# Layer 0 in one-pass products, experts batch by batch: a two-layer kernel with attention and experts

## The reference

```python
qkv = einsum('bsd,ed->bse', xn, w_qkv) + b_qkv      # 16 heads of 16
attn = softmax(q k^T / 4 + causal); s = (attn v) @ w_out.T + b_out
logits = xn @ router_w.T                            # 8 experts, best 2
w = softmax(top2(logits))
gate  = silu(einsum('nd,edf->enf', xn, w1))         # 256 -> 128
value = einsum('nd,edf->enf', xn, w2)
expert_out = einsum('enf,efd->end', gate * value, w3)
f = sum over the two chosen experts of w * expert_out
```

## Time and profile before

| | us |
|---|---|
| median of 3 runs | 1393.04 |
| lowest, highest | 1392.79, 1396.16 |
| the profiled execution, its own time | 1396.62 |
| its span in the profile | 1394.9 |
| mean granted TensorE clock | 0.979 |

### The profile page before, as it was taken

One profiled execution on the slowest core, in us unless ns is written; L12 is line 12 of the kernel. 1 busy time (PEld: TensorE's weight loads), 2 busy tenths in 40 slices (PEclk: granted clock), 3 DMA queues, 4 the chain that ended last, 5 costly groups with the idle time before them and its releaser, 6 DMA issues. The chain is left out here.

```text
span 1394.9 us, 33366 instructions
## 1 busy us (share of the span) xinstructions
PE 1317.5 (94%) x12564; PEld 1086.2 (78%) x12564; DVE 1119.6 (80%) x2294; ACT 946.3 (68%) x2605; POOL 847.0 (61%) x966
## 2 busy tenths in 40 slices
PE   6999999878999999999999999999999999999985
PEld 3554445667898989898888888889888888888884
DVE  4495646898989888979788988878888878887875
ACT  3105574467787878777877777868777777777664
POOL 8011124338866777576767677577776867676652
PEclk9998999989999999999999999999999999999997
DMA  9910001213111121121121111121112222113011
GB/s 323 167 32 2 5 1 46 77 42 99 39 28 43 35 87 42 28 80 36 39 74 40 41 31 41 43 69 53 27 47 62 62 62 54 55 51 88 17 54 38
DMA packets 61592, 78.84 MB, mean 57 GB/s; under 512 B 6232, under 2 KB 48856, under 8 KB 61432
## 3 DMA queue, kind: packets, MB, share of 16 engines
q1 hardware_dynamic: 56696, 62.41, 17.2%
q0 software_dynamic: 4736, 14.29, 3.7%
...
## 5 line engine op out<-in xcount | busy, mean ns | idle before, releaser
L2029 ACT ACTIVATE XY<-ps 128x512 f16<-128x512 f32 x384 | 219.3, 597 | 64.7 <-PE ps L1274 56.8
L1777 DVE TENSOR_TENSOR ZL<-ps,cst 128x256 f16<-128x256 f32 x384 | 152.3, 415 | 32.3 <-PE ps L1261 27.6
L1687 DVE SCALAR_TENSOR_TENSOR yv<-ps,cw,yv 128x511 f32<-128x511 f32 (+2 forms) x192 | 143.3, 746 | 14.9 <-ACT yv L1966 10.0
L973 PE MATMUL ps<-XH,WVh 128*128 128x256 f32 (+1 forms) x384 | 133.1, 347 | 0.9 <-ACT De L2053 0.8
L973 PE MATMUL ps<-XH,WVl 128*128 128x256 f32 (+1 forms) x384 | 122.5, 319 | 0.0
L973 PE MATMUL ps<-XL,WVh 128*128 128x256 f32 (+1 forms) x384 | 122.5, 319 | 0.0
L2062 ACT ACTIVATE sq<-O 128x128 bf16<-128x128 f32 x256 | 79.4, 310 | 58.5 <-DVE O L1836 21.6
L1271 PE MATMUL ps<-ZL,XY 128*128 128x64 f16 x1536 | 105.2, 193 | 3.4 <-DVE ZL L1777 2.1
L1261 PE MATMUL ps<-XY,LT 128*128 128x64 f16 x1536 | 97.9, 193 | 9.0 <-ACT XY L2029 6.1
L1271 PEld LDWEIGHTS ps<-ZL,XY 128*128 128x128 f16 x1536 | 77.6, 98 | 34.1 <-issue 16.7
L1274 PE MATMUL ps<-XY,ZL 128*128 128x64 f16 x1536 | 104.0, 193 | 0.0
...
## 6 DMA issues: line engine op xcount, KB each, us to landing
RC<-crow SPq DMA_DIRECT2D x128, 128.0 KB
...
WK<-in_WK SPq DMA_DIRECT2D x16, 256.0 KB, 2.7
WO<-in_WO SPq DMA_DIRECT2D x16, 256.0 KB, 2.7
...
KS<-spread SPq DMA_DIRECT2D x12, 256.0 KB, 13.7
QS<-spread SPq DMA_DIRECT2D x12, 256.0 KB, 19.3
...
```

The source lines that it names most:

```text
L973: m = pe.matmul(o, a, b, start=c + k == 0, stop=c == 1 and k == 2)
L1687: m = dve.scalar_tensor_tensor(out=dst[:, k:512], in0=ps[:, bk, 0:512 - k], scalar=cw[:, h, j, 3 - k:4 - k], in1=dst[:, k:512], op0=ALU.mu ...
L1777: leave(dve.tensor_tensor(half(ZL[:, k - 2], k, 0), p, lv(k), ALU.mult), "a", u, k)
L2029: leave(act.activation(changed(u, k), ps[:, bank("b", u, k), :].rearrange("p (c n t) -> p c n t", c=2, t=1 << (k - 1)), ACT.Copy), "b", u, k)
```

## The change

Layer 0's Q, K, V, router and expert up-products become `three` products of fp32r parts. The turned rows are stored as XH and XL, GpSimd splits the weights. V is 256 columns, the router's 8 columns follow it in the same tile; V0 is stored with 17 columns per head, the seventeenth is 1, and `pv` reads 32 columns from a step of 17. x is loaded and normed by batch, Q and K are made by batch, and spreads and stacks follow by batch; QS and KS are laid out by batch, without the memsets of unused rows (the products now read 48 or 50 rows instead of 64). The experts run batch 0 first, then batch 1; each expert's weights (384 KB) are fetched into one of three slots (`fx`), so each expert is fetched twice. Silu is written as tanh: ScalarE takes tanh(z/2), VectorE makes (tanh + 1) z, and a factor 2 goes into the routing weights. In layer 1 the three taps of a convolution are three entries of VectorE's list instead of one. The planner has other costs, a delay of 0.08 between parts on one engine, and other `RANK` and `LATER` tables, so all five orders and the banks are new.

```diff
-                key = int((at + p.later) * (1 / self.GRAIN)), p.rank
+                key = int((at + p.later) * (1 / self.GRAIN)), p.rank, p.no
...
-                q.due = max(q.due, end + self.DELAY[p.eng])
+                q.due = max(q.due, end + (0.08 if q.eng == p.eng else self.DELAY[p.eng]))
...
-    P.add(("rt",), -160, ("PE", 3.6), ("DVE", 0.3), takes=True, gives=("rt",))
-    P.add(("tp", 1), -160, ("DVE", 3.3, (("rt",), "DVE")), ("ACT", 1.5))
+    P.add(("tp", 1), -160, ("DVE", 3.3), ("ACT", 1.5))
     P.add(("tp", 2), -160, ("DVE", 3.0, (("tp", 1), "ACT")))
     for k in range(16):
-        e, b = divmod(k, 2)
+        b, e = divmod(k, 8)
         rank = -100 + 2 * k
-        old = [(("exd", *divmod(k - 3, 2), q), "PE") for q in range(2)] if k > 2 else []
+        old = [(("exd", (k - 3) % 8, (k - 3) // 8, q), "PE") for q in range(2)] if k > 2 else []
         x, y = ("exg", e, b), ("exv", e, b)
-        P.add(x, rank, ("PE", 1.81), ("ACT", 0.62, *old), takes=True, gives=x)
-        P.add(y, rank + 1, ("PE", 1.81), ("DVE", 0.6, (x, "ACT")), takes=True, gives=y)
+        if k > 2:
+            P.add(("fx", k), rank, ("SP", 3.0, *old), ("POOL", 1.75))
+        else:
+            P.add(("fx", k), rank, ("POOL", 1.75))
+        P.add(x, rank, ("PE", 1.4, (("fx", k), "POOL")), ("ACT", 0.5, *old), ("DVE", 0.6), takes=True, gives=x)
+        P.add(y, rank + 1, ("PE", 1.4, (("fx", k), "POOL")), ("DVE", 0.6, (x, "DVE")), takes=True, gives=y)
         for q in range(2):
             z = "exd", e, b, q
-            P.add(z, rank + 2, ("PE", 0.86, (y, "DVE")), ("DVE", 0.8, (("exd", e - 1, b, q), "DVE") if e else (("tp", 2), "DVE")),
+            P.add(z, rank + 2, ("PE", 0.97, (y, "DVE")), ("DVE", 0.8, (("exd", e - 1, b, q), "DVE") if e else (("tp", 2), "DVE")),
...
-    P.add(("stack", 0), -300, ("SP", 20.0))
-    P.add(("stack", 1), -300, ("SP", 26.0, (("stack", 0), "SP")))
+    P.add(("stack", 0), -300, ("SP", 14.0))
+    P.add(("stack", 1), -100, ("SP", 14.0, (("stack", 0), "SP")))
...
-        P.add(("pv", *x), rank, ("PE", 0.87 * part + 0.13, (("mk", *x), "POOL"), last and (last, "PE")), takes=j == 0)
+        P.add(("pv", *x), rank, ("PE", 0.95 * part + 0.18, (("mk", *x), "POOL"), last and (last, "PE")), takes=j == 0)
...
+def plan_taps(P, x, rank):
+    for k in (1, 2, 3):
+        P.add(tap(k, x), rank, ("DVE", 0.66, (x, "ACT") if k == 1 else (tap(k - 1, x), "DVE")), gives=x if k == 3 else None)
...
+            sp.dma_start(xt[:, 0:4], xin[:, 0:4]).then_inc(d_x[0], 16)
             sp.dma_start(wqk, chunked(A["wqk"])).then_inc(d_qk, 16)
-            sp.dma_start(bqk[:], A["bqk"]).then_inc(d_qk, 16)
+            sp.dma_start(cst[:, 0:128], A["cst"][:, 0:128]).then_inc(d_id, 16)
+            sp.dma_start(xt[:, 4:8], xin[:, 4:8]).then_inc(d_x[1], 16)
+            sp.dma_start(bqk[:], A["bqk"]).then_inc(d_bqk, 16)
             sp.dma_start(wv[:], chunked(A["wv"])).then_inc(d_v, 16)
             sp.dma_start(bv[:], A["bv"]).then_inc(d_v, 16)
-            sp.dma_start(rw[:], chunked(A["rw"])).then_inc(d_moe, 16)
-            for c in range(2):
-                sp.dma_start(w1[:, c], A["w1"].rearrange("e (c p) f -> c p e f", p=128)[c]).then_inc(d_moe, 16)
-                sp.dma_start(w2[:, c], A["w2"].rearrange("e (c p) f -> c p e f", p=128)[c]).then_inc(d_moe, 16)
-            sp.dma_start(w3[:], A["w3"].rearrange("e p n -> p e n")).then_inc(d_moe, 16)
-            sp.dma_start(bo[:], A["bo"]).then_inc(d_out0, 16)
-            sp.dma_start(wo[:], A["wo"].rearrange("(g p) n -> p g n", p=128)).then_inc(d_out0, 16)
...
+            sp.dma_start(cst[:, 128:C_END], A["cst"][:, 128:C_END]).then_inc(d_cst, 16)
+
+            def fetch_expert(k):
+                sp.dma_start(exr[:, k % 3, :], A["ex"][k % 8]).then_inc(d_ex[k % 3], 16)
+            for k in range(3):
+                fetch_expert(k)
...
+            def spread_out(b):
+                at = slice(512 * b, 512 * b + 512)
+                for t in (2, 3, 0, 1):
+                    w.wait_ge(*done("qk", t, b))
+                    for k, part in enumerate((CH, CL)):
+                        sp.dma_start(spread[k, 128 * t:128 * t + 128, at], part[:, t, at].bitcast(F32)).then_inc(
+                            d_spread[t // 2, k, b], 16)
...
+                if what == "stack":
+                    if h == 0:
+                        spread_out(0)
+                        stack(0)
+                        spread_out(1)
+                    else:
+                        stack(1)
+                        fetch_small()
+                elif what == "fx":
+                    for q in range(2):
+                        w.wait_ge(*full("exd", (h - 3) % 8, (h - 3) // 8, q))
+                    fetch_expert(h)
...
+            w.wait_ge(d_id, 16)
+            for b in range(2):
+                at = slice(512 * b, 512 * b + 512)
+                for n in range(4 * b, 4 * b + 4):
+                    turn(0, n)
+                w.wait_ge(s_wqs, 1)
+                for n in range(4 * b, 4 * b + 4):
+                    w.wait_ge(*done("ln0", n))
+                for t in (2, 3, 0, 1):
+                    bk = enter("qk", t, b)
                     for c in range(2):
...
+                        m = three(ps[:, bk, :], wqkh[:, c, 128 * t:128 * t + 128], wqkl[:, c, 128 * t:128 * t + 128],
+                                  XH[:, c, at], XL[:, c, at], c)
+                    signal(m, "qk", t, b)
             w.wait_ge(d_cst, 16)
...
+            w.wait_ge(s_wvs, 1)
             for n in range(NT):
                 bk = enter("v0", n)
+                at = slice(128 * n, 128 * n + 128)
                 for c in range(2):
-                    m = pe.matmul(ps[:, bk, :], xnT[:, c, 128 * n:128 * n + 128], wv[:, c, :],
-                                  start=c == 0, stop=c == 1)
+                    m = three(ps[:, bk, 0:264], XH[:, c, at], XL[:, c, at], wvh[:, c, :], wvl[:, c, :], c)
...
+                    k, at = 8 * b + e, slice(512 * b, 512 * b + 512)
+                    bk = enter(*x)
+                    w.wait_ge(s_exs, k + 1)
                     for c in range(2):
-                        m = pe.matmul(ps[:, bk, :], wt[:, c, e, :], xnT[:, c, 512 * b:512 * b + 512],
-                                      start=c == 0, stop=c == 1)
+                        k0 = 128 * c + (256 if what == "exv" else 0)
+                        m = three(ps[:, bk, :], exh[:, k % 3, k0:k0 + 128], exl[:, k % 3, k0:k0 + 128],
+                                  XH[:, c, at], XL[:, c, at], c)
                     signal(m, *x)
                 elif what == "exd":
                     e, b, q = x[1:]
-                    bk = enter(*x)
+                    k = 8 * b + e
+                    bk = enter(*x)
+                    w.wait_ge(d_ex[k % 3], 16 * (k // 3 + 1))
                     w.wait_ge(*done("exv", e, b))
                     for n in (2 * q, 2 * q + 1):
                         m = pe.matmul(ps[:, bk, 256 * (n % 2):256 * (n % 2) + 256],
-                                      hT0[:, (2 * e + b) % 3, 128 * n:128 * n + 128], w3[:, e, :], start=True, stop=True)
+                                      hT0[:, k % 3, 128 * n:128 * n + 128], exr[:, k % 3, 512:768],
...
+                                      V0[:, 4 * b + j, 17 * (4 * g + h):17 * (4 * g + h) + 32],
...
+                dve.tensor_scalar(st[:, n, :], xt[:, n, :], mv[:, 2 * n:2 * n + 1], rs[:, n:n + 1], ALU.subtract,
+                                  ALU.mult).then_inc(s_xn[layer], 1)
...
+            def low_rows(b):
+                for n in range(4 * b, 4 * b + 4):
+                    at = slice(128 * n, 128 * n + 128)
+                    w.wait_ge(s_xh0, n + 1)
+                    leave(dve.tensor_tensor(XL[:, :, at], ps[:, bank("ln0", n), 0:256].rearrange("p (c t) -> p c t", c=2),
+                                            XH[:, :, at].bitcast(F32), ALU.subtract), "ln0", n)
+
+            def low_parts(b):
+                w.wait_ge(d_bqk, 16)
+                for k, t in enumerate((2, 3, 0, 1)):
+                    hi, lo = CH[:, t, 512 * b:512 * b + 512], CL[:, t, 512 * b:512 * b + 512]
+                    w.wait_ge(s_hi, 4 * b + k + 1)
+                    leave(dve.scalar_tensor_tensor(out=lo, in0=ps[:, bank("qk", t, b), :], scalar=bqk[:, t:t + 1],
+                                                   in1=hi.bitcast(F32), op0=ALU.add, op1=ALU.subtract), "qk", t, b)
...
+            normed(0)
+            low_rows(0)
+            normed(1)
+            low_parts(0)
+            low_rows(1)
+            low_parts(1)
...
+                elif what == "exg":
+                    e, b = x[1:]
+                    h_ = hT0[:, (8 * b + e) % 3, :]
+                    w.wait_ge(s_tg, nth("ACT", *x))
+                    leave(dve.scalar_tensor_tensor(out=h_, in0=h_, scalar=1.0, in1=ps[:, bank(*x), :], op0=ALU.add,
+                                                   op1=ALU.mult), *x)
...
+            roots(0)
```

(24 more changed lines are left out.)

380 lines of the change are left out of this document (175 added, 205 removed), and 13 rows, old and new, of tables (LATER, RANK).

## The result

The changed kernel takes 1379.8 us (16 runs, 1374.3 to 1390.0); the kernel before, run beside it 16 times, takes 1392.8. The ratio is 0.991, interval 0.989 to 0.993: 13 us or 0.9% faster, where 31 us were forecast. Which chip the first measurement had is not known. The direction was right and the time lies inside the stated range, but the gain is less than half of the forecast.

What follows compares the result with a forecast made beforehand. TensorE's work was taken to bound layer 0, its waits both ends. Terms -24.6 + 1 - 0.7 + 2 + 1 - 3 - 7 = -31.3 us; against the median this gives 1361.7, rounded 1362 us, range 1343 to 1384.

Steps and rivals of the forecast that it cites:

- V and the router: Layer 0 on TensorE: V with fewer columns saves 7.8 us, the router riding in V's last columns 3.5 us.
- Batch 1's gap at the start: Start of layer 0: batch 1's turning and low parts come behind batch 0's, leaving TensorE idle 2.5 us.
- The table loads: ScalarE in layer 0: tanh shares Exp's table, about 20 loads go; 3 us taken back, bounds 0 and 15.
- Layer 1: Same instructions in a new order: 0 us, bounds 15 gained and 15 lost.
- its rival: VectorE becomes the bound, already busy 43.6 of 58 us from 46 to 104: price 11 us, 1373; chance 0.10.
- the handover, -7: Layer 0 to layer 1: batch 0 finishes early, so layer 1's first products follow directly; 7 us gained, bounds 0 and 21.
- the start, -0.7: Start of layer 0: first product near 11 us gains 3.2, batch 1's wait costs 2.5; net 0.7 us gained.
- Q and K: Layer 0 on TensorE: eight tiles at 1.40 us instead of 1.79, saving 3.1 us.
- the up-products: Layer 0's experts on TensorE: 32 tiles at 1.40 us instead of 1.72, saving 10.2 us.
- late fetches, 2: Layer 0: per-batch expert fetches and GpSimd splits make weights and masks late, costing 2 us.
- the stack transfers starve the experts: Layer 0: expert fetches queue behind stack DMAs; 18 us lost plus 3 for the clock, 1383; chance 0.10.
- the two rivals on the order: Layer 1: the new order helps, 1347, chance 0.12; or hurts, 42 us, 1403, chance 0.06.

Runs made afterwards that it cites:

- the later measurements: Changed kernel rerun without edit, twice: 1372.7 and 1370.6 us, ratios 0.9964 and 0.9947 to the kernel before, which takes 1376.6 to 1377.1 us.
- both edits: Changed kernel with batch 0's layer norm earlier on VectorE and GpSimd, and GpSimd's WV splits later: 1366.5 us, ratio 0.9923 to the kernel before.
- the two runs with batch 0 early: Against the version with three edits, batch 0's output products, norm and turns moved earlier, at once or behind batch 1's first scores: 1371.8 and 1365.2 us.
- the version with three edits: Changed kernel with reordered handover norms and WV splits, two GpSimd waits at the start and four expert slots: 1359.1 and 1358.7 us.
- the run with the tables of before: Changed kernel's instructions ordered with the old kernel's RANK and LATER tables: 1388.7 us, ratio 1.0082 to the kernel before.

## Why the prediction was wrong

**Right.** V and the router: -11.4 us for -11.3, by the 0.12 us spacing. Batch 1's gap at the start: 2.2 for 2.5 us. The table loads: gone, worth 4 to 6 for 3. Layer 1: nothing, in the later measurements. VectorE was not the bound where its rival had it (47.5 of 58 us busy from 46 to 104).

**The step that failed: the handover, -7.** It said that "batch 0 can be through its output product, norm and `ln1` before batch 1's last". It measured +6.2, by 13.2 us the largest error. The order of the changed kernel does not do this: all eight output products still run in one row behind the last attention step. What the runs showed in its place has two parts. First, a collision that the prediction did not name: WV's splits on GpSimd lie beside VectorE's chain of adds. Setting them late brings the 13.8 us down to 9.1, and with both edits to 8.4, so 5.4 us of the 13.2. Second, the 7 us were not to be had by the means that the prediction named: the two runs with batch 0 early do what its sentence says, and lost 13 and 6 us. In the first, the last attention rows come 5.7 us late for the output products, and in the version with three edits batch 0's products fill that time. Work that already covers a wait is not saved by moving it. This does not show that no order gains here: batch 0's low parts, behind batch 1's adds on VectorE, were left where they stand in the version with three edits, where TensorE waits 6.71 us for them.

**Mis-sized: the start, -0.7.** The prediction priced eight scalings at 0.41 us from the earlier trace rows, where GpSimd ran only a memset. They took 8.8 us for 3.3, beside the splits of wqk, of V's weights and of the experts. The page "VectorE: DVE Perf Modes" of the Trainium skill (the perf-mode tier table) would have had them an estimated 1.6 us shorter than the old ones; with no split beside them they are 0.5 us shorter (1.38 for 1.63 a set of four). The first product came 2.9 us late. The experts began at 38.2 instead of 31: the other 4 us are Q and K at half the pace, which the prediction put at nothing.

**Mis-sized, and cancelling: Q, K and the rest of the work.** Q and K cost 0.9 us more where 3.1 less was forecast, and the up-products missed 1.9 us; `pv` and `sc` came out 2.3 and 3.9 us below their terms. `pv` shows nothing of the 1 us taken for its new stride. For `sc` the prediction put nothing. From 104 to 135 us, where its first products lie, the granted clock was 0.82 and 0.73 before (104 to 120, 120 to 135) and is 1.00 after. So part of the clock that the prediction hoped to get back with the table loads appears to sit in this line and not among the idle terms. The near-equality of the sums, -24.0 for -23.6, is luck.

**Mis-sized: late fetches, 2.** This rival (the stack transfers starve the experts, 18 + 3 us) was right in kind, and small. In most profiles TensorE waits 2.2 to 3.9 us for one expert, near 57 or near 80 us. The fourth slot removes most of it, worth some 2 us, which the time alone does not resolve.

**Not part of the forecast.** In the first measurement layer 1 with the tail was 5.7 us shorter, which hid as much of the shortfall; in the others it was not. Of the two rivals on the order neither is shown for this change; the run with the tables of before shows that either could have been.

With all three losses undone the gain is 18 us. Of the 13 us that lack to the 31, 7.8 are the handover (8.4 us where 0.6 was forecast). What remains no run took apart; 18.3 us are idle in layer 0, of which 2.2 are XL of batch 1 and 2.1 the exponential behind silu's table load, against 16.3 in the kernel before.
